# A recommendation tower on one core: other order of the first and last tiles, and one-hot units read in three pieces

## The reference

```python
e = jnp.stack([tbl_0[ids[:, 0]], ..., tbl_25[ids[:, 25]]], axis=1)
combined = jnp.concatenate([e, r_dense_x[:, None, :]], axis=1)
interact = jnp.einsum('bfd,bgd->bfg', combined, combined)
z = interact[:, _TRIU_I, _TRIU_J]
h = jnp.concatenate([z.reshape(z.shape[0], -1), r_dense_x], axis=1)
h = jnp.maximum(h @ W_top1 + b_top1, 0.0)      # 479 -> 512
h = jnp.maximum(h @ W_top2 + b_top2, 0.0)      # 512 -> 256
y = h @ W_top3                                 # 256 -> 1
```

## Time and profile before

| | us |
|---|---|
| median of 3 runs | 365.47 (365.24 to 366.26) |
| profiled execution | 367.2 |
| its span, first to last instruction | 365.5 |
| TensorE busy | 333.9 (91%) |
| GpSimd busy | 261.3 (72%) |
| VectorE busy | 184.6 (50%) |
| ScalarE busy | 178.6 (49%) |

### The profile page before, as it was taken

How to read it: one execution, slowest core, us unless ns; L and a number is a source line. 1 busy time by engine, 2 the same in 40 slices (tenths; PEclk the granted TensorE clock), 3 DMA queues, 4 the chain that set the end, 5 groups by cost and what they waited for, 6 DMA issues and landing times.

```text
span 365.5 us, 12436 instructions
## 1 busy us (share of the span) xinstructions
PE 333.9 (91%) x5536; PEld 274.7 (75%) x5536; DVE 184.6 (50%) x439; ACT 178.6 (49%) x234; POOL 261.3 (72%) x265
## 2 busy tenths in 40 slices
PE   1999889698999999999999999989999999988876
PEld 0488768486887888877887888867888788867675
DVE  3699954535356635465356645564365653321322
ACT  2499731544535834284435835265334835273412
POOL 6778877777777777777777777777777777777200
PEclk9999999879999999999999999999999999999999
DMA  7979493243243333334143333234243212222100
GB/s 233 344 216 250 114 299 105 54 107 95 54 124 82 81 95 95 85 79 124 52 126 86 79 94 98 78 81 115 62 121 92 66 48 73 54 52 60 37 4 3
DMA packets 19657, 37.59 MB, mean 103 GB/s; under 512 B 5557, under 2 KB 8501, under 8 KB 19604
## 3 DMA queue, kind: packets, MB, share of 16 engines
q1 hardware_dynamic: 11412, 20.00, 18.8%
q0 software_dynamic: 8192, 16.79, 17.4%
HBM read 36.77 MB, written 0.01 MB: 101 GB/s over the span
## 4 chain that ended last, share of the span: by engine, by line
POOL 47%; PE 31%; issue 16%; DMA 3%; ACT 2%; DVE 0%; DVEq 0%
POOL rows L276 47%; PE ps_lk L588 10%; PE ps_gram L614 6%; PE ps_mlp L641 3%; PE ps_zt L641 3%; DMA rows<-in_tbl,gather_ids 3%; PE ps_tr L599 3%; PE ps_zt L648 1%; PE ps_mlp L648 1%; PE ps_lk L661 1%; ACT xt L414 1%; DMA gather_ids<-in_ids_gather 1%; PE ps_lk L676 1%; PE ps_tr L676 1%; PE ps_zt L628 0%
## 5 line engine op out<-in xcount | busy, mean ns | idle before, releaser
L276 POOL DMA_INDIRECT rows<-in_tbl,gather_ids x256 | 260.0, 1016 | 78.8 <-issue 76.8
L311 DVE TENSOR_SCALAR onehot<-ids 128x512 fp32r<-128x512 f32 (+1 forms) x328 | 126.1, 440 | 74.1 <-PE ps_lk L588 41.3
L588 PE MATMUL ps_lk<-onehot,table 128*128 128x512 f32 (+1 forms) x704 | 156.3, 376 | 4.7 <-DVE onehot L311 3.6
L588 PEld LDWEIGHTS ps_lk<-onehot,table 128*128 128x128 f32 x704 | 121.3, 192 | 26.7 <-issue 4.0
L424 ACT COPY xt<-ps_tr 128x512 f32<-128x512 f32 x64 | 76.9, 1202 | 107.7 <-PE ps_tr L599 107.6
L614 PEld LDWEIGHTS ps_gram<-xt 128*26 128x26 f32 x4096 | 44.3, 103 | 23.1 <-issue 19.0
L614 PE MATMUL ps_gram<-xt 128*26 128x26 f32 x4096 | 53.7, 192 | 8.3 <-issue 3.9
L325 DVE STREAM_TRANSPOSE zs<-ps_gram 128x832 f32<-128x832 f32 x16 | 16.8, 1050 | 74.2 <-PE ps_gram L614 74.2
L411 ACT COPY xt<-ps_lk 128x512 f32<-128x512 f32 x35 | 42.0, 1235 | 20.5 <-issue 9.8
L599 PE MATMUL ps_tr<-ident,rows 128*128 128x128 f32 x256 | 39.4, 276 | 5.1 <-DMA rows<-in_tbl,gather_ids 3.3
L599 PEld LDWEIGHTS ps_tr<-ident,rows 128*128 128x128 f32 x256 | 30.1, 140 | 12.0 <-issue 5.8
(11 more groups left out here) (55 smaller groups left out, 139.3 us busy)
## 6 DMA issues: line engine op xcount, KB each, us to landing
ids<-in_ids_onehot SPq DMA_DIRECT2D x41, 256.0 KB
rows<-in_tbl,gather_ids POOLq DMA_INDIRECT x256, 3.1
w<-in_tbl SPq DMA_DIRECT2D x6, 512.0 KB, 6.8
zt<-in_tbl SPq DMA_DIRECT2D x3, 512.0 KB, 7.0
dense_x<-in_dense SPq DMA_DIRECT2D x8, 128.0 KB
zt<-in_dense SPq DMA_DIRECT2D x8, 128.0 KB, 2.4
h<-in_tbl SPq DMA_DIRECT2D x1, 512.0 KB, 6.0
w<-in_w SPq DMA_DIRECT2D x1, 512.0 KB
```

The costliest lines, as they stand in the source:

```text
L276: pool.indirect_dma_start(rows[n % ROW_BUFS][:, r, :], None, t_[f"tbl_{GATHERED[r]}"], bass.IndirectOffsetOnAxis(ap=gather_ids[:, n, r:r + ...
L311: nc.vector.tensor_scalar(onehot[:, k, 0:w], ids[e % IDS][:, 0:w].bitcast(F32), float(k), None, ALU.is_equal).then_inc(s_unit, 1)
L588: m = nc.tensor.matmul(ps_lk[e % LB][:, x], table[:, i, part, k, :], onehot[:, k, x], start=(k == 0 and j == 0 and part == 0), stop=(k == ...
```

## The change

The first table is treated like the others: its cast and its subtraction are made in two halves, between the first units, and `lookup(0)` uses high and low parts. Twenty matmuls of the identity run ahead of it on TensorE. The raw tables use five staging buffers in turn. Later in chunks 0 and 1 turns, Gram products, one lookup in two halves, units and packing change places, and on ScalarE casts and shifts do. From chunk 1 on, the ids of a step lie in three pieces, each with one element of padding behind it, and a unit reads 3 x 171 elements and writes 513 in a row, one column more than the lookup reads. `finish` keeps its intermediate in the PSUM bank that it reads, and what reuses the bank waits for its end (`s_y`) and not its first half (`s_kept`). In the last tile a part of `last1` moves ahead of the Gram products.

```diff
+THIRDS = 3
+PIECE = -(-N // THIRDS)
+IDS_W = THIRDS * (PIECE + 1)
+UNIT_W = N + 16
...
+def cols_of(e):
+    c, w, tables = STEPS[e]
+    n = w * P * len(tables)
+    if c == 0:
+        return list(range(n))
+    piece = -(-n // THIRDS)
+    return [i // piece * (piece + 1) + i % piece for i in range(n)]
...
-            def make_units(e):
-                dve.wait_ge(s_from, e + 1)
-                for k in range(KT):
+            def make_units(e, ks=range(KT)):
+                if ks[0] == 0:
+                    dve.wait_ge(s_from, e + 1)
+                for k in ks:
...
-                    nc.vector.tensor_scalar(onehot[:, k, 0:w], ids[e % IDS][:, 0:w].bitcast(F32), float(k), None, ALU.is_equal
+                    if STEPS[e][0] == 0:
+                        to, of = onehot[:, k, 0:w], ids[e % IDS][:, 0:w]
+                    else:
+                        piece = -(-w // THIRDS)
+                        to = onehot[:, k, 0:THIRDS * piece]
+                        of = ids[e % IDS][:, 0:THIRDS * (piece + 1)].rearrange("p (t w) -> p t w", t=THIRDS)[:, :, 0:piece]
+                    nc.vector.tensor_scalar(to, of.bitcast(F32), float(k), None, ALU.is_equal
...
+            def low_first(part):
+                k = slice(part * KT // FIRST_PARTS, (part + 1) * KT // FIRST_PARTS)
+                dve.wait_ge(s_high, part + 1)
+                nc.vector.tensor_tensor(table[:, 0, 1, k, :], raw[0][:, k, :],
+                                        table[:, 0, 0, k, :].bitcast(F32), ALU.subtract).then_inc(s_low, 1)
...
-                nc.vector.tensor_tensor(kept[:, :], bank[:, 0:H2], bias2[:, :], ALU.max).then_inc(s_kept, 1)
+                nc.vector.tensor_tensor(bank[:, 0:H2], bank[:, 0:H2], bias2[:, :], ALU.max).then_inc(s_kept, 1)
                 dve.wait_ge(s_kept, n + 1)
-                nc.vector.tensor_tensor_reduce(kept[:, :], kept[:, :], w3[:, :], 1.0, base[:, :], ALU.mult, ALU.add,
+                nc.vector.tensor_tensor_reduce(bank[:, 0:H2], bank[:, 0:H2], w3[:, :], 1.0, base[:, :], ALU.mult, ALU.add,
                                                y[:, n:n + 1]).then_inc(s_y, 1)
...
+            def warm_up():
+                for _ in range(WARM_UP):
+                    nc.tensor.matmul(ps_zt[:, 0:P], ident[:, :], ident[:, :], start=True, stop=True)
...
-            lookup_first()
+            warm_up()
+            lookup(0)
...
             last1(0, 1)
             turn(a + 1, 3)
+            last1(0, 2)
             gram(a + 1, 0)
-            last1(0, 2)
             gram(a + 1, 1)
             last1(0, 3)
```

More of the change, by code:

```diff
@@ L84 @@
 LEAD = (0, 2, 6, 12, 20)
-SPLIT = list(range(1, NO)) + [0]
+FIRST_PARTS = 2
+WARM_UP = 20
 LAST = (CHUNKS - 1) * MLP_USES
@@ L107, in build @@
         dense_x = sb("dense_x", [P, CS])
-        ids = [sb(f"ids{b}", [P, N], I32) for b in range(IDS)]
-        onehot = sb("onehot", [P, RING, N], F32R)
+        ids = [sb(f"ids{b}", [P, IDS_W], I32) for b in range(IDS)]
+        onehot = sb("onehot", [P, RING, UNIT_W], F32R)
         table = sb("table", [P, NO, 2, KT, D], F32R)
@@ L358, in _ @@
             nc.vector.tensor_copy(first[:, :], first_i[:, :]).then_inc(s_first, 1)
-            make_units(0)
+            make_units(0, range(0, 4))
+            low_first(0)
+            make_units(0, range(4, 6))
+            low_first(1)
+            make_units(0, range(6, KT))
             for e in range(1, STEP0[1]):
-                for n in range(len(STEPS[e][2])):
-                    low(STEPS[e][2][n] - 1)
+                for j in STEPS[e][2]:
+                    low(j)
                 make_units(e)
-            low(NO - 1)
             dve.wait_ge(s_const, 3)
@@ L393, in _, with high_first, high @@
         def _(act):
-            def high(n):
-                j = SPLIT[n]
+            def high_first(part):
+                k = slice(part * KT // FIRST_PARTS, (part + 1) * KT // FIRST_PARTS)
+                act.wait_ge(s_raw[0], 16)
+                nc.scalar.copy(table[:, 0, 0, k, :], raw[0][:, k, :]).then_inc(s_high, 1)
+            def high(j):
                 act.wait_ge(s_raw[j], 16)
@@ L559, in _, with lookup @@
         def _(pe):
[L560 to L565, removed]
-                    if k % USE == USE - 1:
-                        m.then_inc(s_unit_used, 1)
-            def lookup(e):
+            def warm_up():
+                for _ in range(WARM_UP):
+                    nc.tensor.matmul(ps_zt[:, 0:P], ident[:, :], ident[:, :], start=True, stop=True)
+            def lookup(e, ks=range(KT)):
                 c, w, tables = STEPS[e]
-                if e >= LB:
+                if e >= LB and ks[0] == 0:
                     pe.wait_ge(s_lk, e - LB + 1)
-                if c == 0:
-                    pe.wait_ge(s_low, tables[-1])
-                elif e == STEP0[2]:
-                    pe.wait_ge(s_low, NO)
-                for k in range(KT):
+                if 0 < e < STEP0[1]:
+                    pe.wait_ge(s_low, split_count(tables[-1]))
+                for k in ks:
+                    if e == 0 and k % (KT // FIRST_PARTS) == 0:
+                        pe.wait_ge(s_low, k // (KT // FIRST_PARTS) + 1)
                     if c == 0:
@@ L701, in _ @@
             gram(0, 1)
+            lookup(e + 1)
             turn(1, 3)
-            lookup(e + 1)
+            lookup(e + 2, range(0, KT // 2))
             gram(1, 0)
-            lookup(e + 2)
+            lookup(e + 2, range(KT // 2, KT))
+            turn_pairs(0)
             gram(1, 1)
@@ L727, in _ @@
                     turn(a, 3)
-                gram(a, 0)
-                lookup(f)
+                    lookup(f)
+                    gram(a, 0)
+                else:
+                    gram(a, 0)
+                    lookup(f)
                 turn(a + 1, 0)
```

73 lines of the change are left out of this document (38 added, 35 removed).

## The result

The changed kernel takes 369.85 us, median of 4 runs (369.10 to 371.21), beside 365.87 us for the kernel before on the same chip: ratio 1.0114, 95% interval 1.0079 to 1.0150. It is slower by about 4 us where 4.4 us less were forecast. The profiled execution takes 369.1 us, its span 367.3 us.

The account below looks back on a forecast made before the run. GpSimd's gathers were taken to bound the kernel up to tile 4, TensorE alone from there. The terms -4.3 - 1.6 + 2.5 - 1.1 + 0.1 = -4.4 us gave 361.1 us from the median of 365.47, range 357.2 to 365.4.

Parts of the forecast that it names:

- units at 0.68 us: One-hot units from chunk 1 on: each unit of 513 elements, read in three pieces, takes 0.68 us.
- gathers at 0.94 us: GpSimd's gathers after about 45 us: no longer held by the units beside them, 0.94 us each.
- the wait at tile 10: TensorE's wait for rows at tile 10's last turn: it goes, -1.6 us.
- `finish` in PSUM at nothing: `finish` in place releases its banks about 0.5 us later: nothing but about +0.1 us at the last one.
- The wait for units in the second lookups: Second lookup of chunks 2 to 6: TensorE waits 0.5 us each for slower units, +2.5 us, bounds 0 and 5.
- The end ... -1.1 us: Last tile: `last1(0, 2)` fills the 1.30 us wait ahead of the Gram products, so the last output comes 1.1 us earlier.
- the two halves of the Gram products follow one another directly: Last tile: no gap between the Gram halves, the chain to the last output starts behind them; part of the -1.1 us.
- -4.3 us at `turn(4, 3)`: Tile 4's last turn: rows come 3.9 us earlier, plus 0.4 us of slack; the rest of TensorE's gain becomes waits.
- The term for the head: First tiles: reordered work and a split first lookup put TensorE alone about 9 us earlier at tile 3.
- 6 with a late warm-up: First tiles: TensorE alone only 6 us earlier at tile 3 if the 20 warm-up matmuls end late.
- the clock's: Rival: TensorE's clock falls at waits for rows, perhaps at `turn(4, 3)`; price 2.9 us, 364.0 us; chance 0.12.
- The slower rival: Rival: one-element-per-cycle units still hold the gathers, and longer; 368.1 us; chance 0.10.

Follow-up runs that it names:

- `tail_back`: The changed kernel with last1(0, 2) put back between the two halves of the last Gram products; 368.56 us, ratio 1.0069 to the kernel before.

## Why the prediction was wrong

For the profiled execution 362.8 us were forecast and 369.1 measured, 6.3 us more: 2.3 up to `turn(4, 3)`, -0.8 from there to `turn(15, 3)`, 4.8 behind it. The forecast median, 361.1 us, is missed by 8.7; the other 2.4 are how far the two profiled executions stand from their medians, and no trace explains them.

Steps that held: units at 0.68 us and gathers at 0.94 us; the wait at tile 10; `finish` in PSUM at nothing. From `turn(4, 3)` to `turn(15, 3)` it had -1.6 + 2.5 = +0.9 us; measured is +0.1. The wait for units in the second lookups is there: in this stretch TensorE's weight loads waited for `onehot` 5 times, 0.5 us at the longest, 2.4 us in all. The matmuls show no idle time of their own for it, so how much of it TensorE lost is open.

**"The end ... -1.1 us" failed.** The gap ahead of the Gram products went from 1.30 to 0.41 us, nearly as said. But "the two halves of the Gram products follow one another directly" assumed that TensorE issues 512 instructions as fast as it can run them. The border 5 instructions into the run left a whole block of products behind it, and the next block was cut off in the same way: 2.31 + 1.80 us of stops against 1.27, and from 350.80, behind the first of them, half clock for 6.8 us, in which the rows of `last2`, `dense_rows` and `last1(0, 3)` take 2.07 + 1.39 + 1.44 us against 1.13 + 0.83 + 0.83 at full clock (the rows of the kernel before, and of `tail_back` for the last). That is 2.8 + 2.1 = 4.9 us, about the tail's difference from the forecast, 4.8 (+3.8 against -1.0). The kernel before showed the sign: 1.27 us of "issue" in the middle of its own last products (351.67 above), for which I had no cause and which I left out of the sum.

**"-4.3 us at `turn(4, 3)`" gave 2.0.** The term for the head took the 1.30 us ahead of tile 2's products as won, and did not ask what the 20 warm-up matmuls do beside taking time: their 40 matmuls with 40 loads move every later border by 80 instructions. One came to lie behind the 104th matmul of `gram(2, 0)`: 2.60 us, and 1.6 us by the low clock (3.52 against 1.90). Without that stop the step is right in mechanism and nearly in size: `turn(4, 3)` at 113.19 and, with GpSimd's wait gone, at 112.39, forecast 112.2, with a wait for rows right ahead of it. In the run with 64 instructions TensorE stood there from 110.36 (113.19 less the wait of 2.83); in the changed kernel 114.49 less 2.60 and 1.6 gives the same 110.3. That is 6.2 us ahead of before, where about 9 were forecast for TensorE alone, 6 with a late warm-up. A wait of 2.59 us for rows at `turn(1, 1)`, 43.83, was not in that sum. At `turn(4, 3)` it should count for little, since tile 4's rows came only 4.1 us earlier and TensorE would have waited for them; no run shows it apart.

Of the rivals, the clock's came true, at another place: it fell behind the stops (2.60 and 2.31 us) and behind the wait of 2.59 us at `turn(1, 1)`, and in the run with 64 instructions behind the wait for rows of 2.83 us that the rival named, to 0.59 over the next 3.8 us. The slower rival (units that hold gathers) is refuted by 0.938 us. No case of mine had TensorE's own instruction stream as the limit, so the side was wrong.

Open is what decides when a block is asked for. In the tail its transfer began 1.2 us after the border was passed (345.67 to 346.86), ahead of the stop at 87.26 as late as 6.3 us after it (78.06 to 84.40), 0.8 us after the products had begun; so I can say where a stop can be, and that in the tail a dense block makes one, but not its length ahead of a run. Nor is there a least time for every block: the one from 111.93 to 113.94 was run through in 2.01 us without a stop, since its transfer had ended at 110.28.

## What to carry to other kernels

Where a stop without a releaser stands inside a run of small matmuls, count instructions: if stops lie a multiple of 256 apart, as all 34 did here, borders of instruction blocks are the first thing to suspect, and an edit that adds or drops instructions upstream moves them, at a cost of microseconds that no view of the edited place shows. Mix work that has few instructions and long run time into runs of tiny matmuls, so that no block of 256 consists of them alone. And judge an edit at more than one alignment before its order is blamed or praised: the same order of work measured 1.0114 and 0.9965 with 64 idle instructions, 3.66 us of TensorE's first microseconds, between them.

## What the runs showed of the hardware

- TensorE's instructions came in blocks of 256; a block of Gram products alone was run through in some 1.3 us, while from one border to the next 3.57 and 3.45 us went by in the tail (345.67, 349.24, 352.69). Behind a stop TensorE resumed 1.33 to 1.50 us after the transfer's end in the changed kernel, 1.23 to 1.60 us in all twelve profiles.
- In the first microseconds one of the program's matmuls of 32 columns took 0.23 us (3.66 us for 16) and 0.27 us (8.68 for 32) behind the 20 warm-up matmuls, and 0.44 us (9.17 for 21) where nothing ran ahead; one of 128 columns took 0.34 us there (6.80 us for 20).
- A single-source compare over three pieces of 171 takes 679 ns for 513 elements, one of 512 in a row 426 ns; beside the slow one gathers run at 0.938 us, as if alone.
